# A DiT block on one core: the prologue's order and engines, and where score maxima are taken and turned

## The reference

```python
c6 = silu(c) @ Wc + bc                       # shift, scale, gate, twice
xm = ln(x) * (1 + sc_msa) + sh_msa
q, k, v = xm @ Wq + bq, xm @ Wk + bk, xm @ Wv + bv
y = softmax((q / 16) @ k.T) @ v              # per head, 512 x 512
x = x + g_msa * (y @ Wo + bo)
h = gelu((ln(x) * (1 + sc_mlp) + sh_mlp) @ W1 + b1)
out = x + g_mlp * (h @ W2 + b2)
```

## Time and profile before

| | us |
|---|---|
| runs | 709.73, 710.11, 710.66; median 710.11 |
| the profiled execution | 708.81 |
| its span | 707.0 |
| mean granted TensorE clock | 0.992 |
| prologue, to the first transposed scores of batch 0 | about 50 |
| step 0, step 1 | 72.4, 96.1 |
| a steady step | 79.8 |

### The profile page before, as it was taken

One profiled execution on the slowest core, in us unless ns is written; L12 is line 12 of the kernel. 1 busy time (PEld: TensorE's weight loads), 2 busy tenths in 40 slices (PEclk: granted clock), 3 DMA queues, 4 the chain that ended last, 5 costly groups with the idle time before them and its releaser, 6 DMA issues.

```text
span 707.0 us, 15845 instructions
## 1 busy us (share of the span) xinstructions
PE 670.0 (95%) x6492; PEld 413.5 (58%) x6492; DVE 552.2 (78%) x1019; ACT 404.6 (57%) x485; POOL 242.6 (34%) x179
## 2 busy tenths in 40 slices
PE   7989998889999999999999999999999989999997
PEld 6543345333766448854687448854687436833986
DVE  5988988699977988789867988689867975651673
ACT  7546663576415874288535865278535872388221
POOL 1770015113532036312453036312453122360545
PEclk9999999999999999999999999999999998999999
DMA  8745005410633106330462106230471102021111
GB/s 304 216 105 154 31 32 166 122 62 17 161 97 88 50 32 169 76 120 26 111 154 79 60 32 177 67 121 17 102 172 37 68 36 64 11 83 64 47 31 36
DMA packets 58120, 63.57 MB, mean 90 GB/s; under 512 B 7576, under 2 KB 49070, under 8 KB 58046
## 3 DMA queue, kind: packets, MB, share of 16 engines
q1 hardware_dynamic: 58048, 62.56, 30.7%
HBM read 24.15 MB, written 12.89 MB: 52 GB/s over the span
## 4 chain that ended last, share of the span: by engine, by line
PE 76%; DVE 15%; issue 3%; ACT 3%; POOL 1%; SPq 1%; DMA 1%; ACTq 0%; DVEq 0%; POOLq 0%
PE ps L878 21%; PE ps L824 14%; PE ps L938 13%; PE ps L1014 11%; DVE mx L1285 8%; PE ps L884 6%; PE ps L1093 3%; PE ps L975 2%; PE ps L870 2%; PE ps L1100 1%; PE ps L923 1%; PE ps L983 1%; ACT z L725 1%; ACT prob L759 1%; DVE stats L1205 1%
## 5 line engine op out<-in xcount | busy, mean ns | idle before, releaser
L1285 DVE TENSOR_REDUCE mx<-ps 128x1 f32<-128x512 f32 x512 | 331.1, 684 | 55.2 <-PE ps L884 33.5
L759 ACT ACTIVATE prob<-ps 128x1024 f32<-128x1024 f32 x256 | 249.1, 1022 | 92.4 <-PE ps L878 58.9
L878 PE MATMUL ps<-qst,kst 98*32 98x512 bf16 x1920 | 142.9, 379 | 0.6 <-ACT prob L759 0.6
L938 PE MATMUL ps<-prob,vaug 128*32 128x512 f32 x1024 | 133.7, 594 | 0.7 <-DVE x L1361 0.4
L878 PE MATMUL ps<-kst,qst 96*32 96x512 bf16 x1348 | 128.6, 381 | 5.3 <-DVE mx L1285 4.4
L688 POOL TENSOR_TENSOR hl<-z,hh 128x512 fp32r<-128x512 f32 x63 | 85.1, 1352 | 125.6 <-DVE hh L1500 125.5
L809 ACT ACTIVATE z<-ps,bias_t 128x512 f32<-128x512 f32 x64 | 43.8, 687 | 127.0 <-PE ps L1014 112.2
L878 PEld LDWEIGHTS ps<-qst,kst 98*32 98x32 bf16 x1920 | 52.6, 97 | 67.8 <-issue 27.1
L878 PEld LDWEIGHTS ps<-kst,qst 96*32 96x32 bf16 x1348 | 37.3, 94 | 78.9 <-DVE mx L1285 48.2
L824 PE MATMUL ps<-w_hi,hh 128*128 128x256 f32 x256 | 73.8, 288 | 0.3 <-POOL hl L688 0.3
L824 PE MATMUL ps<-w_lo,hh 128*128 128x256 f32 x256 | 72.2, 282 | 0.0
(11 more groups left out here) (152 smaller groups left out, 937.8 us busy)
## 6 DMA issues: line engine op xcount, KB each, us to landing
qst<-prob SPq DMA_DIRECT2D x72, 128.0 KB, 3.8
kst<-prob SPq DMA_DIRECT2D x72, 128.0 KB, 3.8
y_scratch<-rb SPq DMA_DIRECT2D x28, 256.0 KB, 2.0
xd<-in_x_dram SPq DMA_DIRECT2D x8, 512.0 KB, 4.0
xa<-in_x_dram SPq DMA_DIRECT2D x7, 512.0 KB, 4.6
yc<-y_scratch SPq DMA_DIRECT2D x14, 256.0 KB
rb<-r_scratch SPq DMA_DIRECT2D x14, 256.0 KB
out_dram<-xn SPq DMA_DIRECT2D x7, 512.0 KB, 3.2
```

What stands on the lines that cost most here:

```text
L759: act.activation(prob[:, s % 2, 2 * p:2 * p + 2, :], ps[:, 2 * p:2 * p + 2, :], ACT.Exp, scale=1.0 / DH).then_inc(exp_done, 1)
L878: m = pe.matmul(out[32 * n:32 * n + 32, :], weights[:, 32 * n:32 * n + 32], moving, start=True, stop=True, skip_group_check=True)
L938: m = pe.matmul(ps[32 * q:32 * q + 32, 4 + g % 2, :], vaug[par][:, kt, G * g + q, :], prob[:, s % 2, q, :], start=kt == 0, stop=kt == TT - ...
L1285: dve.tensor_reduce(mx[(i + 1) % 2][:, t, at_column:at_column + 1], ps[:, BANK_OF[q], :], AXX, ALU.max).then_inc(max_done, 1)
```

## The change

Prologue:
- TensorE transposes batch 0 ahead of the modulation's turn; VectorE normalises ahead of `add_c6`. Idle products ahead of the first Q and K go from 3 and 6 to 2 and 3.
- GpSimd fills half of the -1 rows of `kst`, ScalarE the other half.
- Wq and Wk: the high part is ScalarE's, the low part GpSimd's (both were VectorE's).
- The modulated norm of batch 0 is made by two engines, ScalarE (rounded) and VectorE (full), each on the other's half and then changed over.

Maxima:
- Each turn is issued one block later. In batch 1's first group, split and turn move from the Q/K stage's end to the blocks in mid-Q/K.
- Counts of blocks change in steps 0 and 1 and in the steady MLP; banks 0 and 1 are both open to blocks in every MLP with a next batch (before: bank 1, in steps 1 to 4).
- Step 1: blocks of sub-steps 0 and 1 may use banks 6 and 7; Wo waits for the maxima ahead of it (`AHEAD_OF_WO`); `y_norm` comes one maximum later, the residual a sub-step later, norm pieces are spread otherwise.
- `load_maxima(1, 0)` and its `maxima_rows` come earlier on the SP queue and on ScalarE.

```diff
-REST_STEADY = 0, (1, 1), 0, (0, 1, 0, 1), (0, 1, 0, 1), (1, 1, 1), (2, 2, 2, 2, 2, 0, 0, 0)
+REST_STEADY = 0, (1, 1), 0, (0, 1, 0, 1), (0, 1, 0, 1), (1, 1, 1), (3, 3, 2, 2, 0, 0, 0, 0)
 C_FIRST = {
-    0: ((4,) * 9 + (3,) + (0,) * 6, (0,) * 9 + (1,) + (4,) * 6),
-    1: ((2, 1, 1, 2, 3, 3, 3, 3) + (0,) * 8, (0,) * 8 + (4, 3, 4, 3, 4, 4, 4, 4)),
+    0: ((5, 5) + (4,) * 7 + (1,) + (0,) * 6, (0,) * 9 + (3,) + (4,) * 6),
+    1: ((3, 2, 1, 1, 4, 4, 3, 3) + (0,) * 8, (0,) * 8 + (3, 3, 3, 3, 3, 4, 4, 4)),
 REST_FIRST = {
-    0: (0, (1, 1), 3, (0, 2, 0, 2), (1, 1, 1, 1), (), (8,)),
-    1: (0, (1, 1), 0, (0, 1, 0, 1), (0, 1, 0, 1), (3, 3, 3), (4, 4, 4, 4, 3, 0, 0, 0)),
+    0: (0, (2, 2), 3, (0, 2, 0, 0), (1, 1, 1, 1), (), (3,)),
+    1: (0, (1, 1), 0, (0, 1, 0, 1), (0, 1, 0, 1), (3, 3, 3), (6, 6, 5, 5, 0, 0, 0, 0)),
-TURN_BEHIND = {BLOCKS * b + group_blocks(b, g): (b, g) ...
+TURN_BEHIND = {BLOCKS * b + group_blocks(b, g) + 1: (b, g) ...
-                    blocks(n, (6,), (6,))
+                    blocks(n, (6, 7) if s < WO_FIRST else (6,), (6,))
-        blocks(sum(up) + sum(down), (6, 7, 1) if 1 <= i <= 4 else (6, 7))
+        blocks(sum(up) + sum(down), (6, 7, 0, 1) if i > 0 else (6, 7))
-IDLE_START, IDLE_ATTENTION = (10, 2, 3, 6), (0, 0)
+IDLE_START, IDLE_ATTENTION = (10, 2, 2, 3), (0, 0)
...
+            pool.memset(kst[0][MROW:KROWS, 0:NH // 2, :], -1.0).then_inc(krows_half_set, 1)
+            def query_weights():
+                w = slice(0, 2)
+                pool.wait_ge(xn_done[0], 1)
+                pool.wait_ge(w_split, 1)
+                pool.tensor_tensor(wqkvo[1][:, w]..., stage[:, 0, 0:1024], wqkvo[0][:, w]..., ALU.subtract).then_inc(w_split, 1)
...
                     norm(0, 0)
+                    query_weights()
                     value_weights()
                     norm(0, 1)
...
+            act.wait_ge(wqkvo_loaded[0], 32)
+            act.activation(wqkvo[0][:, 0:2]..., stage[:, 0, 0:1024], ACT.Copy).then_inc(w_split, 1)
+            def first_modulate():
+                act.wait_ge(tp_done[0], 1)
+                act.wait_ge(mod_set, 2)
+                for k in range(KC):
+                    if k:
+                        act.wait_ge(z_done[0], 1)
+                    act.activation(zh[0][:, k, :], ps[:, 2 + k, :], ACT.Identity, ...).then_inc(zh_done[0], 1)
...
+            def first_modulate():                      # VectorE
+                dve.wait_ge(tp_done[0], 1)
+                dve.wait_ge(mod_set, 2)
+                for k in (1, 0):
+                    if k == 0:
+                        dve.wait_ge(zh_done[0], 1)
+                    dve.tensor_scalar(z[0][:, k, :], ps[:, 2 + k, :], ..., ALU.mult, ALU.add).then_inc(z_done[0], 1)
...
                     pe.wait_ge(yh_done, b + 2 if final(b) else b + 1)
+                    if b == 0:
+                        pe.wait_ge(max_done, AHEAD_OF_WO)
```

More of the change, by code:

```diff
@@ L109, in rest_blocks @@
     return REST_FIRST.get(i, REST_STEADY)
-TURN_BEHIND = {BLOCKS * b + group_blocks(b, g): (b, g) for b in ROW_ENDS for g in range(row_groups(b))}
+TURN_BEHIND = {BLOCKS * b + group_blocks(b, g) + 1: (b, g) for b in ROW_ENDS for g in range(row_groups(b))}
 SPLIT_BEHIND = {BLOCKS * b + group_blocks(b, g) - 1: (b, g) for b in range(NB) for g in range(row_groups(b))}
@@ L146, in score_banks @@
                 if i == 1 and s <= WO_FIRST + 1:
-                    blocks(n, (6,), (6,))
+                    blocks(n, (6, 7) if s < WO_FIRST else (6,), (6,))
+                    if s == WO_FIRST - 1:
+                        ahead_of_wo = block
                     continue
@@ L160, in score_banks @@
     assert block == BLOCKS * NB
-    return bank_of, before
+    return bank_of, before, ahead_of_wo
 WO_FIRST, WO_BANKS, WO_FIRST_BANKS = 2, (4, 5), (5, 7)
-BANK_OF, BEFORE = score_banks()
+BANK_OF, BEFORE, AHEAD_OF_WO = score_banks()
 def rows_behind():
@@ L545, in step @@
                 elif runs(i, 2):
+                    if i == 0:
+                        load_maxima(1, 0)
                     fill_stack(i + 2, 0, (0,) if i == 0 else (0, 1, 2))
@@ L853, in turn_modulation @@
                 m.then_inc(mod_turned, 1)
-            idle(IDLE_START[0], 7)
-            pe.wait_ge(silu_done, 3)
-            modulation((0,))
-            idle(IDLE_START[1], 7)
-            turn_modulation(1, 0, 4)
-            pe.wait_ge(bias_loaded, 64)
-            nb = 3 * KC + JT
-            pe.transpose(ps[:, 1, 0:nb], stage[0:nb, 1, 1792:1920], ident[0:nb, 0:nb]).then_inc(bias_turned, 1)
-            idle(IDLE_START[2], 7)
             def transposes(n, b, bank):
@@ L871, in transposes @@
                 m.then_inc(tp_done[n], 1)
+            idle(IDLE_START[0], 7)
+            pe.wait_ge(silu_done, 3)
+            modulation((0,))
+            idle(IDLE_START[1], 7)
+            transposes(0, 0, 2)
+            turn_modulation(1, 0, 4)
+            pe.wait_ge(bias_loaded, 64)
+            nb = 3 * KC + JT
+            pe.transpose(ps[:, 1, 0:nb], stage[0:nb, 1, 1792:1920], ident[0:nb, 0:nb]).then_inc(bias_turned, 1)
+            idle(IDLE_START[2], 7)
             block_at = [0]
@@ L1068, in step @@
                     pe.wait_ge(part_m, 4 * (i + 2))
-                    transposes(0, i + 2, 2)
+                    if later(i, 2, 1):
+                        transposes(0, i + 2, 2)
                 if has_c:
@@ L1251, in set_modulation @@
                 dve.tensor_scalar(mod[:, 2 * scale:2 * scale + 2, :], mod[:, 2 * scale:2 * scale + 2, :], 1.0, None, ALU.add).then_inc(mod_set, 1)
-            def query_weights():
-                w = slice(0, 2)
-                src = stage[:, 0, 0:1024]
-                dve.wait_ge(wqkvo_loaded[0], 32)
-                dve.tensor_copy(wqkvo[0][:, w].rearrange("p n c f -> p (n c f)"), src).then_inc(w_split, 1)
-                dve.wait_ge(w_split, 1)
-                dve.tensor_tensor(wqkvo[1][:, w].rearrange("p n c f -> p (n c f)"), src,
-                                  wqkvo[0][:, w].rearrange("p n c f -> p (n c f)").bitcast(F32), ALU.subtract).then_inc(w_split, 1)
+            def first_modulate():
[4 more added lines that the diff above has]
+                        dve.wait_ge(zh_done[0], 1)
+                    dve.tensor_scalar(z[0][:, k, :], ps[:, 2 + k, :], mod[:, 2 * SC1 + k, 0:1], mod[:, 2 * SH1 + k, 0:1],
+                                      ALU.mult, ALU.add).then_inc(z_done[0], 1)
             for t in range(TT):
@@ L1396, in step @@
                             row_max(i, 1)
-                        if n == 0 and i == 1 and s == 1:
+                        if n == 1 and i == 1 and s == 1:
                             for part in range(3):
@@ L1406, in step @@
                                     norm_piece(0, i + 2, xa, k)
-                    if i == 1 and s == WO_FIRST:
+                    if i == 1 and s == WO_FIRST + 1:
                         residual(0, WO_FIRST_BANKS)
```

30 lines of the change are left out of this document (19 added, 11 removed).

## The result

The changed kernel took 703.41 us (median of 6 runs, 701.41 to 704.22) against 709.92 for the kernel before in the same session (708.81 to 711.10). The ratio is 0.9905, 95% interval 0.9888 to 0.9921: 6.5 us faster by the medians. The forecast was 698.6, its range 694.5 to 704.5. It has the right sign and the range holds the time, but the sum had 11.5 us and 6.5 came. The profiled execution took 702.91 (its span 701.1), where the sum had 697.3 for the execution.

What follows compares the result with a forecast made beforehand. Steady steps were taken as bound by TensorE, steps 0 and 1 as near VectorE's limit with TensorE waiting. Terms summed to -11.5 us: 697.3 for the profiled execution, 698.6 for the median, range 694.5 to 704.5.

Steps and rivals of the forecast that it cites:

- Prologue, -0.7: Start to step -1's first scores: Wv and Wo's high part and all behind it 0.7 us earlier (bounds -1.4, +4.6).
- Step -1's turn, -0.3: Turn of batch 0's first maxima: issued a block later, its 0.31 us wait goes, 0.3 us less (0 to -0.6).
- VectorE has that block when the turn is done: Step -1: a further block ahead of the turn keeps VectorE supplied, so the 0.31 us wait goes.
- Step 0's first exponential 1.0 us earlier: Listed sign that the forecast holds: step 0's first exponential starts 1.0 us earlier.
- Step 0, -0.5: Batch 0's attention: +0.5 us for blocks added to its first two sub-steps, -1.0 for shorter waits at two turns.
- Its end, -4.2: Step 0's end: 16 blocks not 21, turn in mid-Q/K, V at full clock; batch 1's first transposed scores 4.2 us earlier.
- Step 1 to sub-step 4, -1.7: Step 1's start: sub-step 4 comes 13.5 us behind batch 1's first transposed scores, not 15.2; 1.7 us less.
- Sub-steps 4 to 15, -1.4: Step 1's later attention: one block fewer, norm pieces unpiled, the turn's 2.05 us wait mostly gone; 1.4 us less.
- No longer pile: Claim within step 1's sub-steps 4 to 15: norm pieces no longer pile on sub-steps 6 and 7.
- Rest of step 1, -0.5: Step 1 behind attention: three blocks more (0.65 us), but four banks and earlier last maxima; 0.5 us less (+1 to -2).
- Steady steps, -2.2: Steps 2 to 6: the turn's 0.44 us wait goes in each of five steps; 2.2 us less (0 to -2.4).
- "slower" one: Rival: half clock settles in sparse stretches the change makes; seven cancel the gain, eight give 714 us; chance 0.05.

Runs made afterwards that it cites:

- e1: Changed kernel plus nine identity products ahead of the turn of batch 0's first maxima; 702.11 us, ratio 0.9896.
- e11: Kernel before plus identity products in three idle TensorE stretches (first turns of batches 0 and 1, step 6); 707.32 us, ratio 0.9964.
- e3: Changed kernel plus idle products ahead of batch 0's first turn, and second copies and idle products behind V in step 0; 700.45 us, ratio 0.9879.
- e6: e5 plus VectorE's normalisation of step 1's input norm moved from sub-steps 13 and 14 to 14 and 15; 700.94 us, ratio 0.9874.
- e8: Kernel before plus the change's steady part alone (blocks 3, 3, 2, 2 and four banks from step 2); 707.50 us, ratio 0.9977.
- e5: Changed kernel with batch 0's first turn in its old place and the fill behind step 0's three whole blocks; 701.53 us, ratio 0.9887.
- e7: e5 with ScalarE's eviction of batch 1's first maxima and their load put back where the kernel before had them; 705.65 us, one run.
- e4: Changed kernel with only batch 0's first maxima turned where the kernel before turned them; 701.17 us, one run.
- e10: Changed kernel with old first turn, all fills and later normalisation, plus GpSimd's constant-row fill written as 32-bit words; 697.13 us, ratio 0.9828.

## Why the prediction was right, and where it was off

- **Prologue, -0.7:** right to within 0.3 in every link up to 17.5 us (VectorE normalised from 8.79, not 8.5, as the fill had held it back), about -0.5 in the end. The first scores started at 28.45, 28.94 and 28.66 in the three traces of the kernel before and its variants, and between 27.74 and 28.79, mean 28.14, in the eleven with the change. One trace can't tell this term; the DMA's landing varies by more.
- **Step -1's turn, -0.3:** wrong in sign. "VectorE has that block when the turn is done" holds, but the turn itself came 0.7 later and 0.3 of that stayed (e1), and the half clock added 0.94 in the profiled run. "Step 0's first exponential 1.0 us earlier" failed with it: it came 0.9 later (51.44, 50.54 before).
- **Step 0, -0.5:** measured -0.39. **Its end, -4.2:** -4.34, of which the part at 112.7 to 116.1 at half clock in the kernel before makes 1.6 (e11's 22.41), so that 2.8 are left at equal clock; and the cause was only partly the one named. The forecast had counted the return of the full clock in V as certain.
- **Step 1 to sub-step 4, -1.7:** 13.78 behind instead of 15.18 at full clock, so -1.4; in the profile of after +0.87, by the clock.
- **Sub-steps 4 to 15, -1.4:** the turn's wait fell as said (2.05 to 0.78 in e3), but moving the norm pieces put one under GpSimd's sum, and -0.8 came (34.27, 35.06 before); e6 gives 0.74 more back. "No longer pile" looked at VectorE's load alone.
- **Rest of step 1, -0.5:** +0.3, by the crowding.
- **Steady steps, -2.2:** 79.4 in steps 3 to 5 as said, but 79.69 in step 2, where the steady part alone gave 79.38 (e8); why is open. That the five steps came out at -2.45 is luck in part. In step 6 (75.14, 76.28 before) the half clock lasted 3.4 us and not 6.8; e3 and e5, with the same steady part and 6.8 of it, took 75.8. Without this 0.7 the term is -1.8.

So of the 5.0 us missing from 11.5 some 3.2 are the clock: 1.6 that the sum counted as won at step 0's end, and 1.6 that the changed kernel lost by its lower mean clock. The rest, 1.8, lies in terms too large at full clock: the turn that comes later, the normalisation under GpSimd's sum, the crowded blocks and step 2. (The stages give 2.8 for these, as they give 7.1 for the whole where the lines give 8.1.) The time is inside the range because the range is 10 us wide; the sum itself was 5 off.

Of the rivals the "slower" one named the true mechanism and, of the two places in the profiled run, one: the stretch from 115.4 to Wo. The other, the first turn at 45, it did not name; about step -1's first scores, which it named too, the clock fell in e5 and e7. It was given as one that needs seven stretches to matter; the question was not whether it turns the sign, but that such stretches belong into the sum as a mixture. At the chance seen at the first turn (four of eight traces) and the 0.94 measured there they shift the mean, not the sign. The estimate of 1.9 for 4 us fits the stretch that it was read from, but is too high for the new ones: 1.55 for the 3.4 us up to 116.1 (e11), 0.94 for the 3.4 from 45.2, 2.27 for the 6.8 from 120.3. The Trainium skill (TensorE: Matmul & The Clock Gate, "Terms") puts the penalty at half of the throttled time; none of these stages reaches it, and the measurement decides. That VectorE and ScalarE set part of the pace there is the likely reason; it was not tested.

## What to carry to other kernels

A stage that gets shorter because an engine waits less elsewhere can leave TensorE sparse, and its clock then falls in some executions: read the granted clock ahead of the gain, and where idle stretches like these (0.9 to 2.5 us here) can't be removed, put products in them whose result nobody reads, and compare runs at equal clock. When a work list is moved on one engine, look at what GpSimd does at the new time, not only at the engine's own load. And when a result leaves a bank earlier, follow who stands behind that bank before calling the move free.

## What had not been expected of the hardware

- Whether the clock falls behind the same instructions differs from run to run: in e4 it stayed at 1.00 behind the turn, in e5 it was 0.57 from 46 to 50, and in e6, again with the same instructions up to there, 0.51 from 45.5 to 52.4. The time followed the mean granted clock at 0.48 us for 0.001 over 44 runs of one kernel; 0.001 of the mean is 1.4 us at half clock in 709, so each microsecond there costs a third of one on average; the three stretches measured singly cost 0.28, 0.33 and 0.45 of their length (0.94 of 3.4 us, 2.27 of 6.8, 1.55 of 3.4).
- Not weighed beforehand: a GpSimd instruction that only writes held VectorE back too. An operation on 128x16 numbers took 0.85 instead of 0.18 and ended with the fill (4.30 + 0.85 = 5.15, 1.61 + 3.51 = 5.12); with the shorter fill of e10 it took 0.18.
- That fill's time went by element: 4,096 of bf16 took 3.51, 2,048 of 32 bits over the same bytes 1.80.
